# First eight blocks with all rows on ScalarE, gathers alone on GpSimd, later loads of x, in a two-layer GNN kernel

## The reference, cut to what matters

```python
h = jnp.maximum(_layernorm(x, axis=-1), 0.0)                 # x: 100000 x 128, f32
x = x + _L0_gnn_ref(h, edge_index, W_self, b_self, W_neigh, b_neigh)
h = jnp.maximum(_layernorm(x, axis=-1), 0.0)
x = x + _L1_gnn_ref(h, edge_index)

def _L0_gnn_ref(x, edge_index, ...):
    row, col = edge_index[0], edge_index[1]                  # 125000 edges: 100000 loops, 25000 links
    out = x @ W_self.T + b_self
    agg = segment_sum(x[col] @ W_neigh.T + b_neigh, row)
    return out + agg / clip(count(row), 1)

def _L1_gnn_ref(x, edge_index):
    src, dst = edge_index[0], edge_index[1]
    norm = deg(dst) ** -0.5, taken at src times at dst
    return relu(segment_sum(x[src] * norm[:, None], dst))
```

## Time and profile before

| | us |
|---|---|
| median of three runs (1183.37 to 1186.17) | 1185.05 |
| the profiled execution | 1182.12 |
| its span, first to last instruction | 1180.3 |
| busy over the span: TensorE / VectorE / ScalarE / GpSimd | 1057.1 / 1057.1 / 1082.5 / 862.4 |
| the same in shares | 90% / 90% / 92% / 73% |
| first gather of x starts / last one starts | 27.8 / 677.4 |
| first gather of the second layer | 722.0 |
| ScalarE busy from 740 to 1160 us (420 us) | 420.00 |

### The profile page before, as it was taken

How to read it: one execution, slowest core, us unless ns; L and a number is a source line. 1 busy time by engine, 2 the same in 40 slices (tenths; PEclk the granted TensorE clock), 3 DMA queues, 4 the chain that set the end, 5 groups by cost and what they waited for, 6 DMA issues and landing times.

```text
span 1180.3 us, 30320 instructions
## 1 busy us (share of the span) xinstructions
PE 1057.1 (90%) x9408; PEld 955.5 (81%) x9408; DVE 1057.1 (90%) x3040; ACT 1082.5 (92%) x2871; POOL 862.4 (73%) x1143
## 2 busy tenths in 40 slices
PE   1388999999999999999999993799999999999998
PEld 1377999999989988989889992688888888888886
DVE  7779989989989989989989853899999999999995
ACT  2378999999989999999999991999999999999997
POOL 4767777777777877777777714888888888888870
PEclk9689999999999999999999997555555555555555
DMA  6325666767666766776667526499999999999994
GB/s 209 120 71 166 209 197 207 222 190 215 190 202 200 197 214 188 208 198 204 208 194 216 186 98 235 133 297 293 291 282 288 288 282 292 281 285 289 288 288 168
DMA packets 82232, 259.39 MB, mean 220 GB/s; under 512 B 19987, under 2 KB 20357, under 8 KB 82117
## 3 DMA queue, kind: packets, MB, share of 16 engines
q1 hardware_dynamic: 58948, 210.86, 57.3%
q0 software_dynamic: 22400, 46.91, 13.7%
q10 hardware_dynamic: 768, 0.20, 0.1%
HBM read 152.93 MB, written 104.37 MB: 218 GB/s over the span
## 4 chain that ended last, share of the span: by engine, by line
ACT 56%; POOL 15%; issue 11%; DVE 7%; PE 7%; DMA 3%; POOLq 0%; ACTq 0%; DVEq 0%
ACT work L739 24%; ACT p_O L739 14%; POOL X L634 12%; ACT p_T L739 6%; ACT area L754 4%; ACT p_c L739 3%; ACT area L749 2%; DMA X<-in_x,IDX 2%; DVE ST L1333 2%; PE p_O L910 2%; ACT sd L717 2%; POOL work L596 1%; PE p_O L922 1%; POOL work L592 1%; DVE p_O L1376 1%
## 5 line engine op out<-in xcount | busy, mean ns | idle before, releaser
L739 ACT ACTIVATE work<-X,shift,scale 128x128 f32<-128x128 f32 x1372 | 564.7, 512 | 1.8 <-DVE shift L1367 1.8
L634 POOL DMA_INDIRECT X<-in_x,IDX x392 | 387.4, 988 | 127.4 <-issue 98.6
L1333 DVE BATCH_NORM_STATS2 ST<-X 128x6 f32<-128x256 f32 x1176 | 408.2, 415 | 26.7 <-DMA X<-in_x,IDX 24.9
L968 PE MATMUL p_O<-work 32*128 32x128 f32 x1984 | 307.0, 436 | 44.4 <-DVE work L1350 24.8
L634 POOL DMA_INDIRECT X<-x_table,IDX x294 | 286.3, 974 | 76.5 <-issue 61.7
L968 PEld LDWEIGHTS p_O<-work 32*128 32x128 f32 x1984 | 263.9, 323 | 87.8 <-ACT work L739 31.1
L910 PE MATMUL p_O<-wnT,area 128*128 128x128 f32 x1568 | 218.0, 283 | 0.0
L922 PEld LDWEIGHTS p_O<-wsT,area 128*128 128x128 f32 x1568 | 207.2, 193 | 7.6
L922 PE MATMUL p_O<-wsT,area 128*128 128x128 f32 x1568 | 207.8, 276 | 0.0
L739 ACT ACTIVATE p_O<-X,shift,scale 128x128 f32<-128x128 f32 x496 | 199.1, 442 | 0.6 <-DVE shift L1367 0.6
L910 PEld LDWEIGHTS p_O<-wnT,area 128*128 128x128 f32 x1568 | 193.0, 194 | 0.3 <-DVE area L1386 0.3
(11 more groups left out here) (173 smaller groups left out, 1191.9 us busy)
## 6 DMA issues: line engine op xcount, KB each, us to landing
x_table<-area SPq DMA_DIRECT2D x98, 528.0 KB
X<-x_table SPq DMA_DIRECT2D x98, 528.0 KB
X<-in_x SPq DMA_DIRECT2D x98, 512.0 KB, 4.6
out_x<-area SPq DMA_DIRECT2D x98, 512.0 KB, 6.9
X<-in_x,IDX POOLq DMA_INDIRECT x392
X<-x_table,IDX POOLq DMA_INDIRECT x294
moved<-held SPq DMA_DIRECT2D x32, 12.2 KB
es<-in_src SPq DMA_DIRECT2D x1, 488.5 KB, 3.5
```

Of the source, the lines that this page charges most:

```text
L634: nc.gpsimd.indirect_dma_start(got(s)[:, k, 0:w], None, table, bass.IndirectOffsetOnAxis(ap=IDX[:, s, k:k + 1], axis=0)).then_inc(gathered ...
L739: last = nc.scalar.activation(o, row(l, s, r), ACT.Relu, bias=shift[:, s, r:r + 1], scale=scale[:, s, r:r + 1])
L968: last = nc.tensor.matmul(outs1[p][g][:, P * col:P * col + P], SEL[1][q, p, part_of, :], H[1][q, p, draw, :], start=False, stop=(half == 1 ...
L1333: last = V.bn_stats(ST[:, s, r:r + 2, :].rearrange("p r k -> p (r k)"), pair.rearrange("p r c -> p c r"))
```

## The change

- `last_row` of the first eight blocks (`FIRST`) is gone from GpSimd; ScalarE normalises all twelve rows of them. GpSimd only gathers until its step 7. The waits on `row_ready` and `row_scaled` are counted from block 8.
- `LOT[0]` is 2, not 5: indices are staged for two blocks at a time.
- SyncE starts to load x only when window 0 has landed; x of blocks 6 to 9 is loaded one by one as the statistics of blocks 1 to 4 are done. GpSimd, ahead of gathering block 6, waits for the end of the check's preparation, whose space it shares.
- The bias is split by GpSimd (sum and two subtractions, ahead of window 0) and ScalarE (three casts).
- On VectorE the digit cuts move behind the table of group 0 (all but one), mixed with the three comparisons; marks and draws of group 1 start beside block 0 (k = -1) and end in step 4, its table stands in step 6; `BEGIN` is moved accordingly.
- `START_AHEAD` has 15 entries in place of 10, and `STARTING` = 7 steps have the order of the start.

```diff
-LOT = (5, 4)
+LOT = (2, 4)
...
-START_AHEAD = (1, 1, 1, 1, 2, 2, 2, 3, 3, 3)
+START_AHEAD = (1,) * 4 + (2,) * 5 + (3,) * 6
+STARTING = 7
+FIRST = 8
...
-    BEGIN = {2: 3, 3: 17, 4: 31, 5: 45, 6: 58}
+    BEGIN = {2: 7, 3: 20, 4: 33, 5: 46, 6: 59}
...
+    def rows_of(i):
+
+        return range(0, ROWS if i < FIRST else ROWS - 1)
...
-        return 1 if k == 2 else next((g for g in BEGIN if BEGIN[g] + 11 == k), None)
+        return 1 if k == 5 else next((g for g in BEGIN if BEGIN[g] + 11 == k), None)
...
+            sp.wait_ge(s_win[0], 16)
             for s in range(EARLY):
                 load(0, 0, s)
...
-            sp.wait_ge(s_facts, 2)
+            sp.wait_ge(s_facts, 4)
             sp.wait_ge(s_digits, 2 * len(CUTS))
             for s in range(EARLY, RING[0]):
+                sp.wait_ge(st_ready[0], s - EARLY + 2)
                 load(0, 0, s)
...
+            pool.wait_ge(s_w, 64)
+            nc.gpsimd.tensor_tensor(bsum[0:1, 0, :], brow[0:1, 0, :], brow[0:1, 1, :], ALU.add).then_inc(s_bsum, 1)
+            for k in range(2):
+                pool.wait_ge(s_bpart, k + 1)
+                nc.gpsimd.tensor_tensor(bsum[0:1, (k + 1) % 2, :], bsum[0:1, k % 2, :], bpart[0:1, k, 0, :], ALU.subtract
+                                        ).then_inc(s_bsum, 1)
...
+                if l == 0 and i == EARLY:
+                    pool.wait_ge(s_found, 2)
+                    pool.wait_ge(s_facts, 4)
+                    pool.wait_ge(s_digits, 2 * len(CUTS))
...
-                    if l == 0:
-                        pool.wait_ge(row_ready, i - RING[0] + 1)
+                    if l == 0 and i - RING[0] >= FIRST:
+                        pool.wait_ge(row_ready, i - RING[0] - FIRST + 1)
...
             def last_row(turn, off):
 
                 i, s, _ = place(0, turn, off)
+                if i < FIRST:
+                    return
...
-            digit(0)
-            digit(1)
+            for k in range(3):
+                act.wait_ge(s_bsum, k + 1)
+                nc.scalar.copy(bpart[0:1, k, :, :], bsum[0:1, k % 2, :].rearrange("p (j d) -> p j d", j=1
+                                                                                  ).to_broadcast([1, GT, D])).then_inc(s_bpart, 1)
             take_codes(0)
-            for n in range(2, 2 * len(CUTS)):
+            for n in range(2 * len(CUTS)):
                 digit(n)
...
-                    if r in (BT - 1, (ROWS - 2, ROWS1 - 1)[l]):
+                    if r in (BT - 1, (rows_of(off)[-1], ROWS1 - 1)[l]):
...
-                starting = off < len(START_AHEAD)
+                starting = off < STARTING
...
-                    normalise(0, turn, off + 1, range(MID, ROWS - 1))
+                    normalise(0, turn, off + 1, rows_of(off + 1)[MID:])
...
-                pe.wait_ge(row_ready, i + 1)
+                if i >= FIRST:
+                    pe.wait_ge(row_ready, i - FIRST + 1)
...
-                if k == -4:
+                if k == -1:
                     marks(1)
-                if k == -3:
+                if k == 0:
+                    read_products()
                     code_links(1)
                     draw(1, 0)
-                if -2 <= k <= 0:
-                    draw(1, 2 * k + 5)
-                    draw(1, 2 * k + 6)
-                if k == 1:
+                if 1 <= k < 4:
+                    draw(1, 2 * k - 1)
+                    draw(1, 2 * k)
+                if k == 4:
                     draw(1, 7)
                     double(1)
-                if k == 3:
+                if k == 6:
                     decode(1)
-                if k == -1:
-                    read_products()
-                if k == 4:
+                if k == 8:
                     add_products()
...
-            cut_digit(0)
-            cut_digit(1)
             marks(0)
...
-            for n in range(3, 2 * len(CUTS)):
+            for n in range(1, 2 * len(CUTS)):
                 cut_digit(n)
-            compare_edges()
+                if n < 4:
+                    compare_edges(n - 1)
...
-            split_bias()
...
-                starting = off < len(START_AHEAD)
+                starting = off < STARTING
```

## The result

The changed kernel takes **1187.08 us** (median, 1183.82 to 1190.53); the kernel before, run beside it, 1183.85 us. The ratio is 1.0025, 95% interval 1.0015 to 1.0035: slower by a quarter of a per cent, where 1172.7 us and a gain of 1% were predicted. The profiled executions have spans of 1180.3 and 1185.8 us, so 5.5 us came in between these two.

What follows compares the result with a forecast made beforehand. GpSimd's chain of gathers was taken to bound the first layer. Terms -3.0 - 11.7 - 4.7 + 6.0 = -13.4 us, less 1 us charged for ScalarE, gave -12.4: 1185.05 to 1172.7 us, range 1165.5 to 1181.

Steps and rivals of the forecast that it cites:

- window 0 sooner: Start: window 0 no longer queues behind x, so GpSimd's first gather comes earlier; -3.0 us (0 to -3.3).
- bias on GpSimd: Setup: the bias subtractions ahead of window 0 on GpSimd are covered; 0, up to +1 us if handovers are slow.
- last rows: Blocks 0 to 7: without its last row a GpSimd block takes 4.99 us, not 6.45; eight times 1.46, -11.7 us.
- table of group 1: GpSimd's wait before 85.72 us goes, as lots of two first need this table for block 14; -4.7 us.
- more lots: 49 copies to IDX in place of 20 on GpSimd, 0.23 or 0.10 us each extra; +6.0 us.
- ScalarE touches GpSimd: Near step 13 GpSimd's chain (131.8) and ScalarE's (131.9) touch; 1 us charged (0 to 5).
- Does ScalarE let it run ahead?: Steps 0 to 13: follows ScalarE's chain; waits of 2.0 us in step 7, 1.3 in step 8, then none; 1 us charged.
- second rival: ScalarE paces the start: 2 us waits in all five steps 7 to 11, ScalarE 7 us later; gain 6, 1179 us; 17%.
- first rival: Staging copies not hidden, with handovers on both sides: 24 extra lots cost 18.5 to 30 us; 1185.7 to 1197; 6%.
- the coincidences in BEGIN: A table and marks share one VectorE step four times, formerly once; three more make 4.3 us, free while GpSimd paces.
- start of ScalarE's chain: ScalarE's first steps: block 0 normalised from 34.7 us, block 7 at 87.4, block 8 near 96.
- the rule: Block 0's gathers: the skill's VectorE-GpSimd port lock would make two more digit cuts cost up to 1.3 us; nil taken.

Runs made afterwards that it cites:

- c_rows0: The changed kernel with STARTING = 12 and 29 lots, and FIRST = 0, so the last rows of blocks 0 to 7 return to GpSimd: 1179.52 us.
- b_lot2: The kernel before with LOT = (2, 4) in place of (5, 4) and nothing else: 1192.24 us, ratio 1.0066.
- a_start12: The changed kernel with STARTING at 12 in place of 7: 1177.49 us, ratio 0.9932.
- the pair without the comparison: The kernel before with VectorE's selection comparison cut to 4 columns from block 2 on, with lots of five (1173.59 us) and of two (1177.98 us).
- the two edits: Each alone on the changed kernel: STARTING = 12, 1177.49 us; 29 lots in place of 49, the 20 removed in the even part, 1181.80 us.
- the kernel with both edits: The changed kernel with STARTING = 12 and 29 lots in place of 49: 1170.68 us, ratio 0.9876.
- the last five versions: STARTING = 12 and 29 lots, plus: sums in step 19, 1167.21 us; BEGIN respaced, 1169.21; comparison halved, 1168.30; all three, 1167.80; these with older START_AHEAD, STARTING = 10, 1166.86.

## Why the prediction was wrong

It forecast 1172.7 us, range 1165.5 to 1181, and the time is 1187.1. By its own steps:

| term | predicted | found | by |
|---|---|---|---|
| window 0 sooner | -3.0 | -3.1 | first gather 24.66 |
| bias on GpSimd | 0 | 0 | window's issue 8.01 for 7.92 |
| last rows | -11.7 | -8.8, in GpSimd's steps -11.8 | c_rows0 |
| table of group 1 | -4.7 | wait gone; 3.0 kept in b_lot2, all 4.7 fit the 17.7 at block 14 | b_lot2, after |
| more lots | +6.0 (5.3 of it in the even part) | +11.0 to +12.2 in the even part | b_lot2, after |
| ScalarE touches GpSimd | +1 | +9.1 at block 20, +9.6 in time | a_start12 |

- **The step that failed first is "Does ScalarE let it run ahead?"** The waits of steps 7 to 11 were foreseen at the right place and for the right reason, but priced as VectorE's work ahead of the statistics ("2.0 us", "1.3; then none"). That price takes for granted that VectorE's step can begin when its last one ends. It began with a product that hung on ScalarE's step before: 3.81 us of idle VectorE ahead of the 1.0 us of links and 1.5 us of sums, and a TensorE at half clock made 2.7 us of the waits, which the prediction doesn't reckon with at all. The waits therefore didn't fade; they were 2.72, 5.30, 2.64, 1.73 and 1.74 us, 14.1 in all against 3.3. Block 13 was normalised from 140.78 and not 129.5, and 9 us of that are in GpSimd's steps (block 20 at 151.89, with the waits gone 142.82). It is the prediction's second rival in kind (7 us of delay and a gain of 6), and larger than that rival.
- **The second is the price of a lot.** 0.23 us for a copy is what the rows give and what the pair without the comparison confirms. What was missing is VectorE's comparison: with it in place a lot cost 0.35 to 0.53 us. Moving GpSimd by 0.2 us in every second step changes how often it starts inside the comparison (between blocks 20 and 97, first operations 13 times before and 20 after, second ones 27 and 17, gathers 9 and 18), and which kind it hits. That this makes the whole difference is argued from the pair, not shown block by block. The first rival ("Dear lots", +18 us for 24) had the sign and a wrong mechanism, a handover on both sides; without the comparison the handovers cost no more than the row says.
- **What the two explain.** Between profiled executions the miss is 18.0 us (1169.7 forecast, 1187.69 measured). By the prediction's own terms block 20 should be gathered at 140.8; it is 11.1 us later, and `STARTING` = 12 gives 9.1 of them back. The even part is 6.9 us longer than with copies of 0.23. In medians the miss is 14.4 us, 3.6 less, because the profiled execution of the kernel before lay 2.9 under its median and that of the changed one 0.6 above. That the two edits' 9.6 and 5.3 us also add up to about 14.4 is luck: 4.6 of the 5.3 were in the forecast as the price of these 20 copies.
- **Right:** the start, the free runs of gathers, GpSimd as the pacer of the first layer on both sides of the change, the absence of a wait for SRC, the copies' own 0.23 us, and the coincidences in BEGIN as nearly free. The start of ScalarE's chain was right too: block 7 normalised from 87.28 (87.4 foreseen), block 8 from 96.89 ("near 96").
- **A rule read for the wrong instruction.** What the trace shows: GpSimd's operations and gathers that start inside the 0.68 us comparison are drawn out, the first operations until 0.31 to 0.32 us after its end (19 of 19), the gather at 247.86 by 0.53 us; those beside the scaling and adding of products, of the same length, are not (none of 41). The Trainium skill (SBUF — State Buffer, Who interferes with whom) says that a VectorE instruction with two inputs in SBUF contends with a GpSimd instruction that reads SBUF, and that the one that comes second waits until the first is over; the comparison has two such inputs, the others one and one in PSUM. For GpSimd's arithmetic, the traces agree. For the gathers they do not agree with what the same section infers, that a `tensor_tensor` doesn't hold up the writing of descriptors: from 145 to 660 us gathers of over 1.34 us are 10 in the kernel with both edits, and 5 in the kernel before against 2 without the comparison. The measurement decides. The prediction weighed the rule against the cuts of the setup, where block 0's gathers take 6.02 us against 6.58 before, so that two more cuts cost nothing that shows, and not against the comparison that runs in every step.

Left open: why GpSimd's first operations are shut out through both halves of the comparison and most of its second ones are not; how the waits of steps 7 to 11 part between the root's place and the table work; and how much of the 1.5 to 3.8 us by which the last five versions lie below the kernel with both edits is more than chance.

## What to carry to other kernels

When a change shortens the distance between producer and consumer (here blocks three ahead) and also puts the consumer first in its step, draw the whole loop through all engines; if the loop is closed within one step, its price is the sum of the loop, and both engines show idle time in the same step. Look at the granted clock there too: here TensorE's part of the loop was 2.7 us longer by it. An engine that waits for nobody can still be slowed by a neighbour: read the spread of its durations, not the mean, and look at what the other engine ran when the long ones began. Then a small instruction in the pacer's loop can cost more than its row (here 0.35 to 0.53 us for 0.23).

## What the runs showed of the hardware

- A VectorE comparison of 128 x 512 f32 with both inputs in SBUF (0.68 us) holds up GpSimd's operations and its descriptor writing: without it, GpSimd's last row has mean durations of 456 and 538 ns in place of 574 and 619, and 77 steps are 8.3 to 14.0 us shorter. A first operation that begins during it ends 0.31 to 0.32 us after it (19 of 19 in the changed kernel). Of 41 that begin during VectorE's operations of 0.67 to 0.70 us with one input in PSUM none takes over 0.51 us there.
- Two back-to-back VectorE instructions of half the size shorten the delay of gathers (none over 1.30 us) but not that of GpSimd's first operation (up to 0.97 us: 13 of 13 that begin in the first half end after the second).
- TensorE's granted clock was 0.50 (1.2 GHz) from 98 to 103 us and from 111 to 113 in the changed kernel, behind idle times of 2.50, 2.63 and 2.57 us within 18 us; with `STARTING` = 12 there was one of 2.50 us and the clock was 1.00 from 86 to 145 us. The same 16 and 8 matmuls took 2.08 and 2.05 us at the lower level, 1.16 and 1.14 at the higher.
- Twenty timed runs of the changed kernel lie between 1183.82 and 1190.53 us. The spans of the kernel with both edits and of its five last versions lie between 1164.7 and 1169.7 us, so one span of each can't put them in order.
